# Layer 0 of a four-layer graph network: the own neighbour sum is folded to one lane on GpSimd, and TensorE transposes one lane instead of two

## Reference, cut to what matters

```
mask = adj > 0
m[j,k,:] = relu(h[j] @ W1a + (h[j] - h[k]) @ W1b + b1)          # 192 hidden features
hm[j,:]  = sum over k of mask[j,k] * m[j,k,:]
x[j,:]  += hm[j,:] @ W2 + deg[j] * b2
```

## Time and profile before

| what | value |
| --- | --- |
| median of 3 runs | 1604.89 us (1604.22 to 1605.42) |
| the profiled execution | 1604.63 us |
| its span, first to last instruction | 1602.8 us |
| its mean granted TensorE clock | 0.971 |
| TensorE busy | 1440.3 us, 90% of the span |
| VectorE busy | 1273.2 us, 79% |
| ScalarE busy | 939.7 us, 59% |
| GpSimd busy | 493.8 us, 31% |

### The profile page before, as it was taken

One profiled execution on the slowest core, in us unless ns is written; L12 is line 12 of the kernel. 1 busy time (PEld: TensorE's weight loads), 2 busy tenths in 40 slices (PEclk: granted clock), 3 DMA queues, 4 the chain that ended last, 5 costly groups with the idle time before them and its releaser, 6 DMA issues. The chain is left out here.

```text
span 1602.8 us, 42482 instructions
## 1 busy us (share of the span) xinstructions
PE 1440.3 (90%) x11815; PEld 1117.8 (70%) x11816; DVE 1273.2 (79%) x3215; ACT 939.7 (59%) x2169; POOL 493.8 (31%) x610
## 2 busy tenths in 40 slices
PE   0799999999999999999999999999799997973298
PEld 0577777777777777777777777777688887930298
DVE  6699999998999999999999999988344445878755
ACT  0756665666656566665666556653355554826675
POOL 1233333333333333333333333333111111047400
PEclk9999999999999999999999999999799999987599
DMA  6000000000000000000000000000000000000022
GB/s 139 14 8 9 14 7 7 7 7 13 7 7 7 7 13 7 7 7 7 13 7 7 7 7 7 6 1 1 1 0 0 0 0 1 0 0 1 3 49 53
DMA packets 40749, 18.09 MB, mean 11 GB/s; under 512 B 19396, under 2 KB 40710, under 8 KB 40710
## 3 DMA queue, kind: packets, MB, share of 16 engines
q1 hardware_dynamic: 40178, 17.39, 4.4%
q10 hardware_dynamic: 532, 0.21, 0.1%
HBM read 13.40 MB, written 4.19 MB: 11 GB/s over the span
## 5 line engine op out<-in xcount | busy, mean ns | idle before, releaser
L785 DVE SCALAR_TENSOR_TENSOR acc<-slot_banks,acc 128x768 f32<-128x768 f32 x512 | 488.1, 953 | 44.8 <-PE slot_banks L551 34.5
L849 POOL TENSOR_TENSOR acc<-acc 128x384 f32<-128x384 f32 x128 | 128.0, 1000 | 679.2 <-DVE onediff L779 675.4
L551 PE MATMUL slot_banks<-ac_hi,work 128*128 128x192 f16 x1408 | 263.9, 246 | 0.0
L551 PE MATMUL slot_banks<-ac_lo,work 128*128 128x192 f16 x1408 | 263.8, 246 | 0.0
L697 ACT ACTIVATE hmTa<-bank,unscale 128x128 f32<-128x128 f32 x128 | 47.0, 367 | 360.9 <-PE bank L527 360.9
L551 PE MATMUL slot_banks<-ac_hi,onediff 128*128 128x192 f16 x1024 | 186.0, 247 | 18.8 <-DVE acc L785 12.7
L551 PE MATMUL slot_banks<-ac_lo,onediff 128*128 128x192 f16 x1024 | 184.8, 246 | 0.0
L544 PE MATMUL slot_banks<-ac_hi,ident 128*128 128x384 f16 x512 | 168.0, 328 | 10.1 <-issue 9.5
L544 PE MATMUL slot_banks<-ac_lo,ident 128*128 128x384 f16 x512 | 167.0, 327 | 0.0
L551 PEld LDWEIGHTS slot_banks<-ac_hi,work 128*128 (+1 forms) x1408 | 137.9, 98 | 16.7 <-issue 0.2
L551 PEld LDWEIGHTS slot_banks<-ac_lo,work 128*128 (+1 forms) x1408 | 137.9, 98 | 16.7 <-issue 0.2
(11 more groups left out here) (251 smaller groups left out, 3283.9 us busy)
## 6 DMA issues: line engine op xcount, KB each, us to landing
adj_in<-in_adj_dram SPq DMA_DIRECT2D x32, 256.0 KB, 2.8
out_dram<-acc SPq DMA_DIRECT2D x32, 128.0 KB, 2.0
l1w<-in_L_gnn_W_dram SPq DMA_DIRECT2D x2, 64.0 KB
l1b<-in_L_gnn_b_dram SPq DMA_DIRECT2D x2, 64.0 KB
x_all<-in_x_dram SPq DMA_DIRECT2D x4, 0.2 KB, 12.0
nm_in<-in_nodemask_dram ACTq DMA_DIRECT2D x1, 64.0 KB
w1a<-in_L_gnn_W_dram ACTq DMA_DIRECT2D x1, 48.0 KB
w1b<-in_L_gnn_W_dram ACTq DMA_DIRECT2D x1, 48.0 KB
```

The source lines that it names most:

```text
L551: last = nc.tensor.matmul(unit(pair, t, 1), hot(t), part[:, q, H:2 * H].unsqueeze(1), start=False, stop=(e == 1 and (t % SB == SB - 1 or t ...
L785: nc.vector.scalar_tensor_tensor(out=sums, in0=unit((q + k) % 2, 0, SU), scalar=0.0, in1=sums, op0=ALU.min, op1=ALU.add).then_inc(s_free[k ...
L849: nc.gpsimd.tensor_tensor(acc[:, q, 0:2 * H], acc[:, q, 0:2 * H], acc[:, q, 2 * H:4 * H], ALU.add)
```

## The change

GpSimd folds `acc` twice: lanes 2 and 3 onto 0 and 1 (128x384, now signalling `s_half`), then lane 1 onto lane 0 (128x192, new). The new fold stands behind the first shared fold and ahead of the second one; `s_half` is counted twice a graph. TensorE then turns one lane: one matmul in transpose mode less for the first 128 features, and one less for the other 64. The waits of other engines are as they were. The numbers of lines behind L523 are 3 lower in the changed file until L849.

```diff
-            pair = acc[:, q, 0:2 * H].rearrange("p (t h) -> p t h", t=2)
-            for t in range(2):
-                nc.tensor.matmul(pT[:, 0:N], pair[:, t, 0:N], ident[:, :], start=(t == 0), stop=False, is_transpose=True)
+            nc.tensor.matmul(pT[:, 0:N], acc[:, q, 0:N], ident[:, :], start=True, stop=False, is_transpose=True)
             nc.tensor.matmul(pT[:, 0:N], hm2[:, q % 2, 0:N], part, start=False, stop=True)
-            for t in range(2):
-                nc.tensor.matmul(pT[0:H - N, N:2 * N], pair[:, t, N:H], ident[:, :], start=(t == 0), stop=False,
-                                 is_transpose=True)
+            nc.tensor.matmul(pT[0:H - N, N:2 * N], acc[:, q, N:H], ident[:, :], start=True, stop=False,
+                             is_transpose=True)
...
-            nc.gpsimd.tensor_tensor(acc[:, q, 0:2 * H], acc[:, q, 0:2 * H], acc[:, q, 2 * H:4 * H], ALU.add)
+            own = acc[:, q, :]
+            nc.gpsimd.tensor_tensor(own[:, 0:2 * H], own[:, 0:2 * H], own[:, 2 * H:4 * H], ALU.add).then_inc(s_half, 1)
             shared = acc2[:, q % 2, :]
             nc.gpsimd.tensor_tensor(shared[:, 0:H], shared[:, 0:H], shared[:, H:2 * H], ALU.add).then_inc(s_half, 1)
-            pool.wait_ge(s_half, b + 1)
+            pool.wait_ge(s_half, 2 * b + 1)
+            nc.gpsimd.tensor_tensor(own[:, 0:H], own[:, 0:H], own[:, H:2 * H], ALU.add)
+            pool.wait_ge(s_half, 2 * b + 2)
             nc.gpsimd.tensor_tensor(hm2[:, q % 2, :], shared[:, 0:H], shared[:, 2 * H:3 * H], ALU.add).then_inc(s_hm, 1)
```

## The result

The changed kernel takes 1615.16 us (median of 4 runs, 1614.07 to 1616.75) against 1605.16 us before (4 runs, 1604.22 to 1607.71): a ratio of 1.0065, with a 95% interval of 1.0053 to 1.0077. It is 10.0 us slower; 1617 was forecast. The profiled execution took 1614.07 us, 9.4 more than that of before.

What follows compares the result with a forecast made beforehand. TensorE and VectorE, both nearly full, were taken to bound the kernel by turns within each group of four steps. 31 x 0.63 us lost in step 3 less 32 x 0.22 gained in step 0 gave +12.5, so 1617 us; range 1605 to 1624.

Steps and rivals of the forecast that it cites:

- The lead changes hands: Layer-0 loop: TensorE ahead at its transposes in steps 0 and 2, hidden behind VectorE in steps 1 and 3.
- Turn: TensorE's transposes of the own sum: two matmuls fewer at 0.11 us each, so 0.22 us shorter a step.
- GpSimd 0.43 later: GpSimd's three short folds start 0.55 us apart, 1.10 for 0.67, so `hm2` and the low part come 0.43 us later.
- The one-hot of step 2: VectorE's L773 in step 2, held up by GpSimd's later low part: ends 0.43 us later, near 0.75 us long.
- The compares: VectorE's four L758 in step 3, held up by `hm2` and the low part: 1.6 to 1.9 us, before 1.23.
- rule of turns: VectorE and GpSimd alternate, instruction by instruction, at something they share; the one that waits gets the next.
- The other branch: Step 3: the first compare slips in ahead of `hm2`; delay +0.54 us a group, total +9.7 us.
- +0.63: Step 3: VectorE's compares, third half and the seeds of the shared slots come 0.63 us later, in 31 groups.
- 0.22 for step 0: Step 0: TensorE's shorter transposes count in full, 0.22 us less, 32 times, 7.0 us in all.
- TensorE leading all through: Rival: GpSimd's idle time hides the fold, 128 x 0.22 = 28 us less, 1576; chance 0.04.
- no shared resource: Rival: VectorE stretches but shares nothing with GpSimd; steps 0 and 2 count, 14 us less, 1590; chance 0.06.
- The compares in one piece: Rival: step 3's four compares run together, low part behind them; 11.4 us less, 1593; chance 0.10.

## Why the prediction was right

- **What bounds.** The lead changes hands in a group as said: the turn counted in steps 0 and 2 where only TensorE was edited, 13.8 us for 14.
- **Turn.** 0.22 shorter: L521 starts 0.16 behind L520, L524 0.20 behind L522. The gap of 0.20 stayed. The Trainium skill, "TensorE: Matmul & The Clock Gate", Part 4, with its 275 ns for a transpose would have made this 0.55, by the forecast's estimate; as a price here the distance of starts holds.
- **GpSimd 0.43 later.** 2.61 for 2.17, 0.44. The turn did not wait for `hm2`, with the exception of the last one (3.6 us, and 3.2 before the change).
- **The one-hot of step 2.** 0.75 for 0.32, the 0.43. Step 1's was left alone, as said.
- **The compares.** 1.86 us; 1.91 was forecast (521.76 to 523.67). Their single rows in the change's timeline, the first two of the four:

```profile
525.87 0.67 DVE L755 TENSOR_SCALAR work<-row,end 128x128 f16<-128x128 f16 x1
...
526.46 0.95 DVE L755 TENSOR_SCALAR work<-row,end 128x128 f16<-128x128 f16 x1
```

  The first ends at 526.54, behind `hm2` (526.48), the second at 527.41, behind the low part (527.36); the median of all is 0.24. Here the forecast had some luck. By its rule of turns a compare that waits gets the next one, and the first compare asked 0.05 ahead of the end of a fold; the sum all the same let `hm2` go first, without a reason, and the chip did so. The other branch stood at +9.7 and not +12.5; the measured 10.0 lies nearer to it, although its order did not happen.
- **Sum, where the sizes were off.** From VectorE's third half in step 1 to the seeds of step 3 it was 19.07 us before (524.58 in the earlier trace rows, less the start below) and is 19.57 now (529.21 - 509.64): +0.50, for 0.63. The start before, and the same place two groups on:

```profile
505.51 0.96 DVE L785 SCALAR_TENSOR_TENSOR acc<-slot_banks,acc 128x768 f32<-128x768 f32 x1
...
572.72 0.96 DVE L785 SCALAR_TENSOR_TENSOR acc<-slot_banks,acc 128x768 f32<-128x768 f32 x1
```

  and after:

```profile
577.52 0.96 DVE L782 SCALAR_TENSOR_TENSOR acc<-slot_banks,acc 128x768 f32<-128x768 f32 x1
```

  The term "+0.63" was too large, mostly by two small things. The low part was not held up by the first compare (0.91 as ever), for which I had added 0.05. And the seeds started 0.21 behind the end of the third half before, but 0.15 now (529.21 - 529.06): 0.06 had been slack, which I took for latency. Two groups take 67.88 us (577.52 - 509.64) for 67.21 (572.72 - 505.51): +0.34 a group, for 0.41. So the rest of a group became 0.16 shorter, where the forecast had 0.22 for step 0. The start of step 0's first seeds shows what is missing, before the change and after it:

```profile
526.66 0.33 PE L544 MATMUL slot_banks<-ac_hi,ident 128*128 128x384 f16 x1 [0.26 <-issue]
```

```profile
531.35 0.33 PE L541 MATMUL slot_banks<-ac_hi,ident 128*128 128x384 f16 x1 [0.33 <-issue]
```

  They come 2.08 us behind the shared seeds before (526.66 - 524.58) and 2.14 now (531.35 - 529.21); what they wait for is open. The two errors have opposite signs. By 31, 0.34 makes 10.4 against 12.5, with 9.4 measured in the profiled executions.
- **Where TensorE waits.** I named the seeds. The wait of 0.6 us shows one place ahead in TensorE's list, at the host ranks; both hang on the same compares.
- **Rivals.** TensorE leading all through (1576) and no shared resource (1590) fell with the one-hot's 0.75. The compares in one piece (1593) fell with the second compare's wait: the whole is 1.86 and not under 1.23, and the time did not fall.

Still open: whether the engines alternate or whoever asks first goes first. The first compare, issued at 525.87 with a fold ending at 525.93, lost to `hm2`, issued at 525.89. By strict turns it should have gone ahead of it; by order of asking that needs `hm2` to ask sooner after its issue than a compare does, which no run here measured. The timeline shows an order, `hm2`, first compare, low part, second compare, and no rule for who goes first.

## What to carry to other kernels

An idle engine's time is free only if what it does shares nothing with a busy one. Before work is moved to GpSimd, lay its timeline beside VectorE's and list which VectorE instructions under it take the shared way to SBUF. In these traces they were the compares and one-hots from fp16 rows in SBUF, and a subtraction with two inputs from SBUF; the sums with one input from PSUM and one from SBUF were not held up. Such a clash shows as one instruction of a line with a maximum far above its median, and it can be cheaper to hold GpSimd's next instruction back than to shorten it: here one wait was worth 28 us (ratios 1.0065 and 0.9888).

## What was not expected of the hardware

The price of a clash is what is left of GpSimd's instruction, however short VectorE's is: a compare that takes 243 ns alone took up to 951, and the one-hot and the two compares held up in the change's timelines ended 0.05 to 0.12 us behind the GpSimd instruction beside them. And the taking of turns splits a run of short instructions: two of the four compares waited, 0.67 and 0.95 us, and the four together took 1.86 us, so that the other two went at their usual pace.
The compare read from PSUM takes 0.10 us more each in itself (340 for 243 ns), and was still cheaper beside GpSimd: 1598 against 1615 us (ratios 0.9961 and 1.0065).
